# Four slots instead of two for raw expert weights and for routing rows, and the second half's norm and router spread over more expert steps

## The reference

```
x = x + tanh(g_xattn[0]) * attention_0(x, ctx)        # softmax over ctx x ctx
x = x + tanh(g_ffn[0])   * bitnet_ffn(x)              # 8 bit activations, ternary weights
x = x + tanh(g_xattn[1]) * attention_1(norm(x), ctx)  # 16 heads of 128, q and k RMS-normed
x = x + tanh(g_ffn[1])   * moe(norm(x))               # this is what the change is about

moe(h):  logits = h @ gate_w.T                        # 64 experts
         top 8 of 64, softmax over the 8 -> weight w[token, expert] (0 elsewhere)
         y = sum_e w[:, e] * ((silu(h @ G_e.T) * (h @ U_e.T)) @ D_e.T)   # inner width 64
         y = y + sigmoid(h @ g1) * shared_expert(h)
```

## Time and profile before

| | |
|---|---|
| median of 3 runs | 697.79 us (697.5 to 698.92) |
| profiled execution | 698.7 us, of which 696.9 us is the span |
| PE busy | 628.3 us (90%) |
| DVE busy | 488.3 us (70%) |
| ACT busy | 431.6 us (62%) |
| POOL busy | 211.4 us (30%) |
| DMA moved | 55.30 MB, mean 79 GB/s |
| transfers `raw<-in_expert_w` | 64 of 384 KB, 3.5 us each from issue to landing (median) |
| transfers `w_all<-w_rows` | 128 of 128 KB, 2.9 us each |

### The profile page before, as it was taken

How to read it: one execution, slowest core, us unless ns; L and a number is a source line. 1 busy time by engine, 2 the same in 40 slices (tenths; PEclk the granted TensorE clock), 3 DMA queues, 4 the chain that set the end, 5 groups by cost and what they waited for, 6 DMA issues and landing times.

```text
span 696.9 us, 11883 instructions
## 1 busy us (share of the span) xinstructions
PE 628.3 (90%) x3652; PEld 527.2 (76%) x3652; DVE 488.3 (70%) x1179; ACT 431.6 (62%) x1083; POOL 211.4 (30%) x200
## 2 busy tenths in 40 slices
PE   6635877999999999999998789899999899999997
PEld 3512566999999999899887668687777677778785
DVE  4899766776776679786866477776667467767665
ACT  4838757988888888768895434443444344444442
POOL 1447162765566666446575010000000000000000
PEclk9959889999999999999999999999999999999999
DMA  8310010212000000000010234345443354545551
GB/s 308 102 46 0 1 46 23 70 47 69 3 1 2 1 1 3 0 3 1 9 54 1 76 89 138 114 153 152 155 151 114 113 162 146 153 153 155 166 151 45
DMA packets 24720, 55.30 MB, mean 79 GB/s; under 512 B 4064, under 2 KB 4704, under 8 KB 24544
## 3 DMA queue, kind: packets, MB, share of 16 engines
q1 hardware_dynamic: 24672, 54.71, 25.2%
HBM read 53.39 MB, written 1.31 MB: 78 GB/s over the span
## 4 chain that ended last, share of the span: by engine, by line
PE 57%; DVE 11%; issue 8%; ACT 6%; DMA 6%; POOL 2%; SPq 2%; DVEq 0%; POOLq 0%; ACTq 0%
PE bank L261 16%; PE bank L263 15%; PE bank L262 15%; DMA raw<-in_expert_w 5%; PE bank L662 3%; PE bank L642 2%; ACT att L1070 2%; ACT front_hi L1204 2%; SPq L311 2%; DVE prod L1573 1%; PE bank L634 1%; DVE inter L1589 1%; PE bank L594 1%; PE bank L697 1%; DVE rowmax L1493 1%
## 5 line engine op out<-in xcount | busy, mean ns | idle before, releaser
L1103 ACT ACTIVATE inter_hi<-inter 128x512 fp32r<-128x512 f32 (+1 forms) x66 | 41.7, 632 | 144.0 <-DVE inter L1589 139.7
L261 PE MATMUL bank<-xnT_hi,front_hi 128*128 128x512 f32 x256 | 104.7, 409 | 9.3 <-ACT gate_s L1099 4.1
L263 PE MATMUL bank<-xnT_hi,front_lo 128*128 128x512 f32 x256 | 102.8, 402 | 0.0
L262 PE MATMUL bank<-xnT_lo,front_hi 128*128 128x512 f32 x256 | 102.6, 401 | 0.0
L1593 DVE TENSOR_TENSOR inter_lo<-inter,inter_hi 128x512 fp32r<-128x512 f32 (+1 forms) x66 | 45.7, 692 | 49.4 <-ACT inter_hi L1103 49.4
L1678 DVE TENSOR_TENSOR front_lo<-raw,front_hi 128x768 fp32r<-128x768 f32 x60 | 57.5, 958 | 26.8 <-ACT front_hi L1204 25.5
L1070 ACT ACTIVATE att<-bank,shift,rq 128x256 f32<-128x256 f32 x128 | 71.3, 570 | 3.7 <-DVE shift L1500 3.7
L427 POOL TENSOR_TENSOR att<-att,rowinv 128x512 f32<-128x512 f32 x64 | 65.9, 1049 | 14.1 <-DVE rowinv L1510 13.9
L1493 DVE TENSOR_REDUCE rowmax<-bank 128x2 f32<-128x512 f32 x64 | 43.8, 685 | 36.7 <-PE bank L263 36.6
L261 PEld LDWEIGHTS bank<-xnT_hi,front_hi 128*128 128x128 f32 x256 | 49.3, 192 | 24.8 <-issue 7.1
L411 POOL TENSOR_TENSOR rk<-msq,minus_half 128x4 f32<-128x4 f32 x32 | 32.4, 1013 | 106.5 <-DVE msq L1482 106.4
(11 more groups left out here) (241 smaller groups left out, 1777.8 us busy)
## 6 DMA issues: line engine op xcount, KB each, us to landing
raw<-in_expert_w SPq DMA_DIRECT2D x64, 384.0 KB, 3.5
w_all<-w_rows SPq DMA_DIRECT2D x128, 128.0 KB, 2.9
raw<-in_head_qk SPq DMA_DIRECT2D x8, 384.0 KB, 3.1
wvo_raw<-in_head_vo SPq DMA_DIRECT2D x8, 384.0 KB, 3.1
gate_raw<-in_gate_wT SPq DMA_DIRECT2D x1, 1408.0 KB, 10.7
x<-in_x_tok SPq DMA_DIRECT2D x2, 512.0 KB, 6.1
outT<-final SPq DMA_DIRECT2D x4, 256.0 KB, 2.1
down_raw<-in_down_wT SPq DMA_DIRECT2D x1, 640.0 KB, 10.9
```

The source lines that it names most:

```text
L261: pe.matmul(out, l_hi, r_hi_, start=start, stop=False, skip_group_check=True)
L262: pe.matmul(out, l_hi, r_lo_, start=False, stop=False, skip_group_check=True)
L263: return pe.matmul(out, l_lo, r_hi_, start=False, stop=stop, skip_group_check=True)
```

## The change

There are four slots for raw weights: the two of `raw`, then `wvo_raw` (free after the attention) and a new tensor `e_more`; `w_all` has four slots. Semaphores, slot numbers and the counts waited for follow. SP may run four pairs ahead, not two. `keep_rows(1)` moves from before load 18 to before load 20, the output transfers from after 6 to after 12 loads of the second half. `turn_weights(0)` and `turn_shared(0)` move one group later, and the second half's norm, router and weights are spread over steps 2 to 14 instead of 2 to 10. DVE's order at the very start of the experts (`low_inter(1, 1)`, `low_e(2)`, `low_e(3)`) is the same. The diff, cut to its core:

```diff
-        w_all = sd("w_all", [P, 2, 512])
+        w_all = sd("w_all", [P, 4, 512])
+        e_more = sd("e_more", [P, 768])
...
+        def e_raw(r):
+            return raw[:, r, :] if r < 2 else (wvo_raw, e_more)[r - 2][:, :]
...
             keep_rows(0)
             sp.wait_ge(t_K, GROUPS)
             for q in range(2):
                 spread_rows(q, q, 0)
-
-            def first_half(q, par):
-                sp.wait_ge(v_Elo, q - 3)
-                load_expert(par, q)
-                sp.wait_ge(v_mul2, q - 1)
-                spread_rows(par, q, 0)
-
+            load_expert(2, 2)
+            sp.wait_ge(t_Y, 2 * (GROUPS - PAIRS + 4))
+            load_expert(3, 3)
             for q in range(2, 4):
-                sp.wait_ge(g_Elo, q - 1)
-                load_expert(q % 2, q)
-                sp.wait_ge(v_mul2, q - 1)
-                spread_rows(q % 2, q, 0)
-            for q in range(4, 18):
-                first_half(q, q % 2)
+                spread_rows(q, q, 0)
+
+            def first_half(q, r):
+                sp.wait_ge(v_Elo, q - 5)
+                load_expert(r, q)
+                sp.wait_ge(v_mul2, q - 3)
+                spread_rows(r, q, 0)
+
+            for q in range(4, 6):
+                sp.wait_ge(g_Elo, q - 3)
+                load_expert(q - 4, q)
+                sp.wait_ge(v_mul2, q - 3)
+                spread_rows(q - 4, q, 0)
+            for q in range(6, 20):
+                first_half(q, q % 4)
             keep_rows(1)
...
+            def second_half(e, r):
+                sp.wait_ge(v_Elo, e + (EPAIRS - 5))
+                load_expert(r, e)
+                sp.wait_ge(v_mul2, e + (EPAIRS - 3 if isinstance(e, int) and e < 4 else EPAIRS - 2))
+                spread_rows(r, e, 1)
+
+            for e in range(12):
+                second_half(e, e % 4)
             for hb in range(2):
                 sp.wait_ge(v_out, hb + 1)
                 sp.dma_start(outT[hb, :, 0:512], final[:, hb, 0, :]).then_inc(l_out, 16)
...
@@ tensor, attention loop @@
-                if g == 25:
+                if g == 26:
                     turn_weights(0, KBK)
-                if g == 26:
+                if g == 27:
                     turn_shared(0, KBK)
...
@@ tensor, experts @@
-            for q in range(2, 12):
+            for q in range(2, 16):
                 step(q % 4, q % 2, 0, q, q)
                 experts_down((q - 1) % 4, (q - 1) % 2, 0, q - 1)
-                if q in (3, 4):
+                if q in (6, 7):
                     pe.wait_ge(v_Tlo, 2 * GROUPS)
-                    turn_rows(2, q - 1, TBK[q - 3])
-                if q == 6:
+                    turn_rows(2, q - 4, TBK[q - 6])
+                if q == 9:
                     router(1, 2)
-                if q == 9:
+                if q == 13:
                     turn_weights(1, 3)
-                if q == 10:
+                if q == 14:
                     turn_shared(1, 2)
-            with pe.Fori(3, EPAIRS // 4) as i:
+            with pe.Fori(4, EPAIRS // 4) as i:
...
@@ scalar, experts @@
-                if q == 7:
+                if q == 10:
                     weight_exps(1)
...
@@ vector, experts @@
-            for q in range(2, 12):
-                step(q, q % 2, q, q + 2, q // 2)
+            for q in range(2, 16):
+                step(q, q % 2, q, q + 2, q // 4)
                 if q == 2:
-                    tile_stats(4, TILES)
+                    tile_stats(4, 6)
+                if q == 3:
+                    tile_stats(6, TILES)
                     ask_rstd(4, TILES)
+                if q == 4:
                     ask_pow()
-                    normalise(4, TILES)
-                if q in (3, 4):
-                    low_rows(2, q - 1, TBK[q - 3])
-                if q == 6:
+                    normalise(4, 6)
+                if q == 5:
+                    normalise(6, TILES)
+                if q in (6, 7):
+                    low_rows(2, q - 4, TBK[q - 6])
+                if q == 9:
                     take_logits(1, 2)
                     choose(1)
-                if q == 8:
+                if q == 11:
                     weights(1)
```

More of the change, by code:

```diff
@@ L127, in flamingo_kernel @@
         l_hvo, l_out = sem("l_hvo"), sem("l_out")
-        l_exp = [sem("l_exp0"), sem("l_exp1")]
+        l_exp = [sem(f"l_exp{i}") for i in range(4)]
         pool_const = sem("pool_const")
@@ L233, in flamingo_kernel @@
         t_wk, a_wk, l_wrows = sem("t_wk"), sem("a_wk"), sem("l_wrows")
-        l_wall = [sem("l_wall0"), sem("l_wall1")]
+        l_wall = [sem(f"l_wall{i}") for i in range(4)]
         t_G, t_U, t_W, t_D, t_F, a_silu, a_Ihi, a_Ehi, v_mul1, v_mul2, v_Ilo, v_Elo, v_out = (sem(n) for n in (
@@ L253, in w_lo @@
             return front_lo[:, p, :] if p < EARLY else back_lo[:, p - EARLY, :]
-        e_hi, e_lo, e_raw = front_hi, front_lo, raw
+        e_hi, e_lo = front_hi, front_lo
+        def e_raw(r):
+            return raw[:, r, :] if r < 2 else (wvo_raw, e_more)[r - 2][:, :]
         block = ctx.enter_context(nc.Block())
@@ L356, in _ @@
                 sp.dma_start(outT[hb, :, 0:512], final[:, hb, 0, :]).then_inc(l_out, 16)
-            with sp.Fori(3, EPAIRS // 2) as i:
-                for par in range(2):
-                    second_half(i * 2 + par, par)
+            with sp.Fori(3, EPAIRS // 4) as i:
+                for r in range(4):
+                    second_half(i * 4 + r, r)
             for hb in range(2):
@@ L1092, in split_e @@
             def split_e(q):
-                act.wait_ge(l_exp[q % 2], (q // 2) * 16 + 16)
-                act.activation(e_hi[:, q % 4, :], e_raw[:, q % 2, :], ACT.Copy).then_inc(a_Ehi, 1)
+                act.wait_ge(l_exp[q % 4], (q // 4) * 16 + 16)
+                act.activation(e_hi[:, q % 4, :], e_raw(q % 4), ACT.Copy).then_inc(a_Ehi, 1)
             def silu(slot, s, rows=P):
@@ L1202, in step @@
                 high_inter(slot, s)
[L1203 to L1204 removed]
+                act.wait_ge(l_exp[(r + 2) % 4], expert_turn * 16 + 16)
+                act.activation(e_hi[:, (r + 2) % 4, :], e_raw((r + 2) % 4), ACT.Copy).then_inc(a_Ehi, 1)
             def last_steps(slot, s, q):
@@ L1243, in _ @@
                     q = i * 4 + (EPAIRS + r)
-                    step(r, (r + 1) % 2, i * 4 + (EPAIRS + 1 + r), q, i * 2 + (EPAIRS // 2 + r // 2 + 1))
+                    step(r, (r + 1) % 2, i * 4 + (EPAIRS + 1 + r), q, i + (EPAIRS + r + 2) // 4)
             for r in range(4):
@@ L1247, in _ @@
                 if r < 2:
-                    step(r, (r + 1) % 2, q + 1, q, q // 2 + 1)
+                    step(r, (r + 1) % 2, q + 1, q, (q + 2) // 4)
                 else:
@@ L1682, in last_steps @@
                 times_up(slot, s)
-                times_loaded(slot, s, r % 2, turn)
+                times_loaded(slot, s, r % 4, turn)
                 low_inter(slot, s)
@@ L1690, in finish @@
                                              xT_end[:, hb, t * 512:(t + 1) * 512], ALU.mult, ALU.add).then_inc(v_out, 1)
-            for q in range(2, 12):
-                step(q, q % 2, q, q + 2, q // 2)
+            for q in range(2, 16):
+                step(q, q % 2, q, q + 2, q // 4)
                 if q == 2:
-                    tile_stats(4, TILES)
+                    tile_stats(4, 6)
+                if q == 3:
+                    tile_stats(6, TILES)
                     ask_rstd(4, TILES)
+                if q == 4:
                     ask_pow()
-                    normalise(4, TILES)
-                if q in (3, 4):
-                    low_rows(2, q - 1, TBK[q - 3])
-                if q == 6:
+                    normalise(4, 6)
+                if q == 5:
+                    normalise(6, TILES)
+                if q in (6, 7):
+                    low_rows(2, q - 4, TBK[q - 6])
+                if q == 9:
                     take_logits(1, 2)
                     choose(1)
-                if q == 8:
+                if q == 11:
                     weights(1)
-            with dve.Fori(3, EPAIRS // 4) as i:
+            with dve.Fori(4, EPAIRS // 4) as i:
                 for r in range(4):
-                    step(r, r % 2, i * 4 + r, i * 4 + (r + 2), i * 2 + r // 2)
+                    step(r, r % 2, i * 4 + r, i * 4 + (r + 2), i)
             times_up(0, EPAIRS, EI)
@@ L1713, in _ @@
                 q, s = EPAIRS + e, EPAIRS + 1 + e
-                step(e, s % 2, s, q + 2, q // 2)
+                step(e, s % 2, s, q + 2, q // 4)
             dve.wait_ge(a_xT, 4)
@@ L1723, in _ @@
                 if r < 2:
-                    step(r, (r + 1) % 2, q + 1, q + 2, q // 2)
+                    step(r, (r + 1) % 2, q + 1, q + 2, q // 4)
                 else:
-                    last_steps(r, (r + 1) % 2, q + 1, q // 2)
+                    last_steps(r, (r + 1) % 2, q + 1, q // 4)
             times_up(1, 2 * EPAIRS + 1, EI)
```

57 lines of the change are left out of this document (25 added, 32 removed).

## The result

The changed kernel takes 686.87 us (median, 685.32 to 687.63, 4 runs) against 697.83 (697.5 to 698.92): ratio 0.9837, 95% interval [0.9817, 0.9858]. It is 11.0 us faster; 12.3 had been forecast. The profiled execution took 687.63 us with a span of 685.8.

A forecast was written before the change was run, and what follows sets the result against it. PE was taken to bound the expert stage at 4.20 us per step. Gains 4.2 + 0 - 0.3 + 7.5 + 0.9 = 12.3 us took the profiled 698.7 to 686.4, hence a median of 685.5; range 681.3 to 690.5 (own range 684 to 687.5).

The forecast's parts named there:

- What bounds: Expert stage: PE never rests, its floor is 4.20 us per step, and only its waits can be won.
- The start of the experts: PE's wait at 396 for `front_lo` of pair 2: gain 0, ends 0 and 2.67 plus a tail of some 1.4.
- Norm: Second half's norm at 409: PE loses 0.7 us in small waits instead of 4.86, gain 4.2 us.
- The ledger: Tally of DVE's lateness over steps 3 to 8 against an allowance of 1.02 us; PE loses 0.7 us.
- Router and weights: Waits at 437 and 442: silu stays 1.46 us, the wait for `chosen` only changes its name; gain 0.
- Attention: First half's weights at 335: wait for `chosen` becomes one for `o_lo`, transposes no longer hidden; net 0.3 us lost.
- Four slots and small waits: Waits at 479, 546 and 576 go, 7.5 us; small waits in the steady steps give 0.9 us.
- SP's order: Waits at 479, 546 and 576 come from SP's issue order: raw loads stand behind rows that wait for inter.
- the spare of 6.6 us: With four slots, time left of 12.6 us after issuing (up to 2.5) and landing (3.5) before ACT wants the load.
- The term for the turn: PE's wait at 546, the turn of the halves, with its slow-clock tail: 3.02 + 1.49 us, all to go.
- Rival 1: Every wait simply vanishes with nothing behind it: 16.3 us gained, so 681.5 us; chance 0.12.
- Rival 4: Slower: SP's streaming into slots DVE reads lengthens DVE's operations; at 25% the kernel takes 707.9 us; chance 0.07.

The follow-up runs named there:

- the two mixed kernels: The changed kernel with four row slots but only two raw slots: 687.01 us; with four raw slots but only two row slots: 692.36 us.
- four slots only: The changed kernel with the norm, router, weights and first half's transposes placed as before: 690.38 us, ratio 0.9920.

## Why the prediction held, step by step

**What bounds.** PE's floor of 4.20 us per step was right to the hundredth over 24 steps, and so was reading gains only from its waits.

**The start of the experts (forecast 0, 1.3 gained).** The wait is the same 2.50 us idle, its tail is not. Where the prediction names two waits with a slow clock behind them there were three, and this is the third; only its last paragraph counts on it. The 3.12 us behind it, the kernel before and then the changed one, PE alone, with the granted clock in the third column from the right:

```profile
395.98:399.10 3.12, 3.12 (x8) 0.55 0.49 144
```

```profile
399.11:402.23 3.12, 3.12 (x13) 1.00 0.49 159
```

Behind this wait of 2.67 us from start to start the clock fell in 5 of 11 profiled executions and stayed in 6, the changed kernel both times among the latter. I had given the tail as an end of the range, not as a gain; nothing in the edit earns it, so this 1.3 us is luck.

**Norm (4.2 forecast, 4.0 measured).** The ledger put the loss at 0.7 us; the gate of step 6 came 0.84 late. It erred in form: I expected several waits of 0.2 to 0.4 us, and there was one of 0.58 idle, because `inter_lo` of step 4 met POOL's last subtraction:

```profile
414.02 0.73 POOL L474 TENSOR_TENSOR sdn_lo<-sdn_raw,sdn_hi 64x256 fp32r<-64x256 f32 x1
414.22 1.08 DVE L1602 TENSOR_TENSOR inter_lo<-inter,inter_hi 128x512 fp32r<-128x512 f32 x1 [0.76 <-ACT inter_hi L1112]
```

`normalise` away from POOL took 403 to 410 ns instead of 401 to 807. Both agree with what the Trainium skill says (SBUF — State Buffer, section "SBUF: two separate sides"), that GpSimd and a VectorE operation with two SBUF inputs or in a two-port mode exclude each other. The operation was 0.39 us longer (up to 0.7 had been named), and moving POOL's work took that away. Without it gate 6 came 0.48 us late and the step behind it took 0.13 more, so DVE's work alone costs some 0.6 us, and the ledger's 0.7 fits.

**Router and weights (0 forecast).** 1.46 us for silu as before, then 0.63 + 0.68 = 1.31 for prod and `inter_lo`, against 0.64 + 0.76 = 1.40 worked out and 1.43 before. Removing the wait on `chosen` gained 0.1 us; its time went to the two others.

**Attention (0.3 lost forecast, 0.33 measured)**, with the wait on `o_lo` at 1.31 us.

**Four slots and small waits (8.4 forecast, 9.03 measured).** The large waits were 7.5 us of it, and all the small ones were gained, 1.5 instead of 0.9. The reason given, SP's order, is shown by the two mixed kernels. To call the spare of 6.6 us ample was right: even with two raw slots ACT never waited for raw weights, given four row slots. The term for the turn, 3.02 + 1.49 us, was read from the one execution with the long issue; two other kernels with two row slots idled 1.67 and 1.62 us there with no slow clock behind. As a measure of the kernel it is some 2.5 us too high.

**The sum.** For the expert steps 12.6 us was forecast and 14.2 came in the traces, 1.3 of it by the clock and 2.5 by the long issue, so some 10.4 is the change's. Between the traces and the median stands what I had no term for: the stretch up to 124 us, which differs by up to 3.1 us between kernels that are equal there. The forecast of 685.5 was 1.4 us low, and it came that near partly by luck: the slow clock (1.3 us) and the small waits (0.6) gave more than forecast, and the first column took back 2.66. The mechanism is shown; the gain by medians is 8.7 to 11.0 us, below the 12.3 of the sum. Rival 1 (every wait simply vanishes) would have been 4 us further down, and the waits that changed their names speak against it. Rival 4 is excluded: L1602 kept its 0.69 us in every step but one, the step with POOL, and the steady step its 4.20.

## What to carry to other kernels

When an engine waits for a transfer, look at what stands before it in its queue's list: here two more slots for the small rows gave everything, and two more for the large buffer that was waited for gave nothing on top. Before a term is taken from one profiled execution, look whether its cause, here a transfer that took 1.40 us to issue, comes in a second one. Before you remove a wait, work out what the same engine would wait for next; two of the named waits here only changed their name. Work that must be squeezed into an engine's steady loop can be planned with a ledger of slack per step and the lateness allowed, and a table load belongs where its engine idles: here moving it there, with `weights(1)` split, gave 2.75 us.

## What was not expected of the hardware

The same 2.50 us idle before the same matmul was followed by the granted clock's lower level of 1.2 GHz in five profiled executions and by 2.4 GHz in six. It is worth 1.3 to 1.6 us, and single profiles of this kernel should not be compared across it.

Of the 128 row transfers of a trace nearly all took 0.47 to 0.60 us to issue, but single ones took 1.40 us (the kernel before), 1.44 (four slots only) and 1.42 (four row slots, two raw slots), and in eight of the thirteen traces none took more than 0.61. No run shows why.
